# One core, attention and mixture of experts: the first layer norm's transposes by DMA, its bias by DMA, and the last row maxima among the attention units

## The reference

```python
x = x + xattn(layernorm(x), ctx_768, Wq, bq, Wk, bk, Wv, bv, Wo, bo)   # 16 heads of 16, softmax over 64 keys
x = x + ffn(layernorm(x), gate_w, shared and expert weights)           # shared SwiGLU + top 2 of 8 experts
```

## Time and profile before

| | |
|---|---|
| time, median of 3 runs (lowest to highest) | 719.77 us (718.18 to 723.15) |
| profiled execution, its own time | 715.89 us |
| its span, first to last instruction | 713.9 us |
| mean granted TensorE clock, as a share of 2.4 GHz | 0.912 |
| busy: PE, DVE, ACT, POOL | 614.5, 440.9, 346.4, 394.1 us |

### The profile page before, as it was taken

How to read it: one execution, slowest core, us unless ns; L and a number is a source line. 1 busy time by engine, 2 the same in 40 slices (tenths; PEclk the granted TensorE clock), 3 DMA queues, 4 the chain that set the end, 5 groups by cost and what they waited for, 6 DMA issues and landing times.

```text
span 713.9 us, 15571 instructions
## 1 busy us (share of the span) xinstructions
PE 614.5 (86%) x5294; PEld 416.7 (58%) x5294; DVE 440.9 (62%) x925; ACT 346.4 (49%) x561; POOL 394.1 (55%) x325
## 2 busy tenths in 40 slices
PE   4687668899978888977599899999999999999990
PEld 2243233566546554544356578877878787878780
DVE  5857886687787745779996644544454444454450
ACT  3797457787759763453224433333343333333330
POOL 5579687987864102121304446465756665666643
PEclk9899885598768998998989999999999999999996
DMA  8500000134212559434314766466656655656533
GB/s 262 176 2 1 0 1 1 32 70 107 42 39 46 141 150 248 142 100 115 96 59 131 159 91 105 69 106 92 106 85 99 103 99 92 108 93 107 91 46 37
DMA packets 103819, 65.08 MB, mean 91 GB/s; under 512 B 78594, under 2 KB 96964, under 8 KB 103748
## 3 DMA queue, kind: packets, MB, share of 16 engines
q1 hardware_dynamic: 88916, 40.86, 24.7%
q0 software_dynamic: 14832, 23.24, 19.3%
HBM read 29.47 MB, written 17.96 MB: 66 GB/s over the span
## 4 chain that ended last, share of the span: by engine, by line
PE 60%; DVE 20%; ACT 6%; issue 5%; DMA 3%; SPq 3%; POOL 2%; POOLq 0%; DVEq 0%; ACTq 0%
PE bank L1414 58%; DVE arena L966 3%; SPq L493 2%; DVE bank L1019 2%; DMA out<-w_stage,map_i 2%; DVE hidden L1299 2%; ACT arena L818 1%; PE bank L1764 1%; DVE arena L1276 1%; DVE arena L1272 1%; POOL arena L583 1%; ACT arena L733 1%; DVE x_sb L1355 1%; DVE bank L1305 1%; DVE arena L931 1%
## 5 line engine op out<-in xcount | busy, mean ns | idle before, releaser
L1414 PE MATMUL bank<-arena 128*128 128x34 f16 (+6 forms) x1284 | 138.1, 253 | 27.3 <-DVE bank L1019 11.4
L1414 PE MATMUL bank<-qx,arena 128*128 128x256 f16 (+1 forms) x1584 | 157.5, 288 | 3.2 <-ACT hidden L793 2.6
L674 POOL DMA_INDIRECT out<-w_stage,map_i x71 | 114.4, 1611 | 71.4 <-DMA out<-w_stage,map_i 32.6
L1414 PEld LDWEIGHTS bank<-qx,arena 128*128 (+1 forms) x1584 | 126.7, 101 | 25.4 <-issue 10.2
L1414 PEld LDWEIGHTS bank<-arena 128*128 128x128 f16 (+2 forms) x1284 | 74.3, 108 | 78.1 <-issue 47.3
L661 POOL DMA_INDIRECT qx<-rows_d,map_i x71 | 71.8, 1011 | 76.6 <-DVE lane_w L1375 33.7
L1383 DVE TENSOR_TENSOR hidden<-bank,hidden 128x512 f32<-128x512 f32 x71 | 49.1, 692 | 104.3 <-ACT hidden L900 104.3
L1414 PE MATMUL bank<-qx,w_sh 128*128 128x512 f16 x384 | 95.7, 399 | 19.8 <-DVE hidden L1299 17.7
L900 ACT ACTIVATE hidden<-bank 128x512 f32<-128x512 f32 x71 | 42.4, 597 | 129.4 <-PE bank L1414 129.4
L1414 PE MATMUL bank<-arena,w_stage 128*128 x852 | 104.6, 273 | 0.6 <-DVE w_stage L1402 0.4
L1414 PE MATMUL bank<-arena,qx 128*128 (+1 forms) x316 | 84.4, 390 | 14.3 <-DVE arena L966 12.6
(11 more groups left out here) (185 smaller groups left out, 725.1 us busy)
## 6 DMA issues: line engine op xcount, KB each, us to landing
w_stage<-in_w_all SPq DMA_DIRECT2D x27, 512.0 KB, 4.4
x_sb<-in_x SPq DMA_DIRECT2D x8, 512.0 KB, 8.1
rows_d<-arena SPq DMA_DIRECT2D x8, 512.0 KB, 4.0
out<-x_sb POOLq DMA_DIRECT2D x8, 512.0 KB, 5.6
qx<-rows_d,map_i POOLq DMA_INDIRECT x71, 3.1
qx<-qx SPq DMA_TRANSPOSE x71, 3.1
out<-w_stage,map_i POOLq DMA_INDIRECT x71, 3.9
arena<-arena SPq DMA_TRANSPOSE x32, 2.5
```

The costliest lines, as they stand in the source:

```text
L674: pool.indirect_dma_start(out=out, out_offset=bass.IndirectOffsetOnAxis(ap=map_i[:, 1, i:i + 1], axis=0), in_=y_sb[:, r], in_offset=None, ...
L1414: return pe.matmul(o, a, b, start=first, stop=last, skip_group_check=not check)
```

## The change

- Groups 2 to 7 of the first layer norm are transposed by DMA from SP (24 `dma_start_transpose`, four a group) straight from `xn_hl`, which holds high and low half side by side and has three buffers in place of two, into `xn_t`. TensorE's transposes and ScalarE's copies remain for groups 0 and 1. SP issues these DMAs ahead of the first four weight loads.
- Scale and shift come in four chains in place of three, and `k_h` is cast after the third. ScalarE normalises three groups ahead in place of two.
- `add_bo` is a DMA from GpSimd's queue that adds the broadcast `bo` from DRAM to `x_sb`; the broadcast through TensorE goes.
- The low halves of `k`, `wo` and `v` are made on GpSimd in place of VectorE. Three of the four low key blocks move into units 0 to 2.
- 48 row maxima are taken ahead of the flag in place of 56; scores 18 to 47 rotate over four banks. Maxima 48 to 55 come in units 0 and 1, four each; 56 to 63 in units 3 to 10, one each, through bank 7. `copy_max` and `max_t` of the last groups move to later units, and so do three weight splits.

```diff
--- before.py
+++ after.py
...
@@ -347,10 +348,45 @@
         block = ctx.enter_context(nc.Block())
 
         N_CONST = 28
-        N_K, N_Q, N_V = 5, 3, 9
-        CHAIN_OF = (1, 2, 2, 2, 3, 3, 3, 3)
-        SCORED = (0, 0, 8, 18, 29, 40, 48, 56)
-        MAX_BANK = (6, 6, 6, 6, 6, 6, 7, 6)
+        N_K, N_Q, N_V = 5, 2, 9
+        CHAIN_OF = (1, 2, 3, 3, 4, 4, 4, 4)
+        SCORED = (0, 2, 8, 16, 24, 32, 40, 48)
+        XN_BY_PE = 2
+        WIDE_FROM, WIDE_TO = 18, 48
+        LATE_MAX = 56
+
+        def max_bank(n):
+
+            return 6 if n < NG - 2 else 7
+
+        def score_bank(j):
+
+            if j >= LATE_MAX:
+                return 7
+            if WIDE_FROM <= j < WIDE_TO and j % 4 >= 2:
+                return j % 2
+            return 4 + j % 2
+
+        def scores_read_for(j):
+
+            if j >= LATE_MAX:
+                return j
+            return j - 3 if WIDE_FROM <= j < WIDE_TO else j - 1
+
+        def xn_transposed(eng, n):
+
+            if n < XN_BY_PE:
+                eng.wait_ge(xt_ready, n + 1)
+            else:
+                eng.wait_ge(xn_got[n % 2], 16 * GT * (n // 2))
+
+        def late_scores(u):
+
+            if u < 2:
+                return range(LATE_MAX - 8 + 4 * u, LATE_MAX - 4 + 4 * u)
+            if 3 <= u < 11:
+                return range(LATE_MAX + u - 3, LATE_MAX + u - 2)
+            return range(0)
 
...
+
+            for n in range(XN_BY_PE, NG):
+                sp.wait_ge(xnl_ready, n + 1)
+                sp.wait_ge(q_ready, HF * (n - 1))
+                for t in range(GT):
+                    sp.dma_start_transpose(xn_t[:, n % 2, :, :, bass.ts(t, P)].rearrange("p s h t -> p (s h) t"),
+                                           xn_hl[:, n % 3, t].rearrange("p a c -> p (a c)")
+                                           ).then_inc(xn_got[n % 2], 16)
...
             def normal_low(n):
 
                 pool.wait_ge(xnh_ready, n + 1)
-                if n >= 2:
-                    pool.wait_ge(xt_ready, n - 1)
-                pool.tensor_tensor(xn_l[:, n % 2], xn[:, n % 2], xn_h[:, n % 2], ALU.subtract).then_inc(xnl_ready, 1)
+                pool.tensor_tensor(xn_hl[:, n % 3, :, 1], xn[:, n % 2], xn_hl[:, n % 3, :, 0],
+                                   ALU.subtract).then_inc(xnl_ready, 1)
 
             def add_bo(n):
 
-                xg = x_sb[:, bass.ts(n, GT), :]
-                pool.tensor_tensor(xg, xg, bo_bc.unsqueeze(1).to_broadcast([P, GT, C]),
-                                   ALU.add).then_inc(bo_added, 1)
+                pool.wait_ge(xn_ready, n + 1)
+                pool.dma_start(x_sb[:, bass.ts(n, GT), :],
+                               bo.rearrange("(a b c) -> a b c", a=1, b=1).to_broadcast([P, GT, C]),
+                               accum_op=ALU.add).then_inc(bo_added, 16)
...
             def keys(c, b):
 
-                pool.wait_ge(kh_ready, c + 1)
+                pool.wait_ge((kh_ready, kl_ready)[c], 1)
...
+            def values_low(h2):
+
+                r = slice(h2 * KV, (h2 + 1) * KV)
+                vf = v_f[r].rearrange("p b (j h d) -> p b j h d", h=2, d=D)[:, :, :, h2, :]
+                vh = v_hh[r].rearrange("p b (j h d) -> p b j h d", h=2, d=D)[:, :, :, h2, :]
+                pool.tensor_tensor(v_blk_l[r, :, :, h2 * D:(h2 + 1) * D], vf, vh,
+                                   ALU.subtract).then_inc(vblk_ready, 1)
+
             pool.wait_ge(const_ready, N_CONST)
             normal_low(0)
             pool.wait_ge(wq_hi, 1)
             pool.tensor_tensor(wq_hl[:, 1], wq_f, wq_hl[:, 0], ALU.subtract).then_inc(wq_lo, 1)
             keys(0, 0)
             normal_low(1)
-            pool.wait_ge(bo_copied, 1)
+            normal_low(2)
             for n in range(NG):
                 query_low(n)
+                if n + 3 < NG:
+                    normal_low(n + 3)
                 if n < B - 1:
                     keys(0, n + 1)
-                elif n < 2 * B - 1:
-                    keys(1, n - B + 1)
-                if n + 2 < NG:
-                    normal_low(n + 2)
-                if n >= 2:
-                    add_bo(n - 2)
-            for n in range(NG - 2, NG):
+                if n == 2:
+                    pool.tensor_tensor(k_l, k_f, k_h, ALU.subtract).then_inc(kl_ready, 1)
+                if n == 3:
+                    keys(1, 0)
+                if n == 4:
+                    pool.wait_ge(wo_hi, 1)
+                    pool.tensor_tensor(wo_hl[:, 1], wo_f, wo_hl[:, 0], ALU.subtract).then_inc(wo_lo, 1)
+                if n == 5:
+                    pool.wait_ge(vh_ready, 1)
+                if n in (5, 6):
+                    pool.wait_ge(ql_ready, HF * (n + 1))
+                    values_low(n - 5)
+                    pool.wait_ge(vblk_ready, n - 4)
                 add_bo(n)
...
 
             def unit(u):
-                if u == 1:
+                if u < B - 1:
+                    keys(1, u + 1)
+                if u == 3:
                     low_weight(1)
...
-                if n >= 2:
-                    act.wait_ge(xt_ready, n - 1)
-                act.copy(xn_h[:, n % 2], xn[:, n % 2]).then_inc(xnh_ready, 1)
+                if n >= 3:
+                    xn_transposed(act, n - 3)
+                act.copy(xn_hl[:, n % 3, :, 0], xn[:, n % 2]).then_inc(xnh_ready, 1)
...
             normal(0)
             project_inputs()
+            normal(1)
             copy_xt(0)
-            normal(1)
+            normal(2)
             for n in range(NG):
                 query(n)
-                if n + 1 < NG:
-                    copy_xt(n + 1)
+                if n == 0:
+                    copy_xt(1)
                 if 1 <= n <= B:
                     copy_v(n - 1)
-                if n + 2 < NG:
-                    normal(n + 2)
+                if n + 3 < NG:
+                    normal(n + 3)
             act.wait_ge(scale_ready, 1)
+            act.wait_ge(vblk_ready, 2)
...
                 if known(u, 0):
                     cast_p(u, RT - 1)
-                if u == 0:
-                    for q in range(3):
-                        split_hi(q)
+                if 1 <= u < 4:
+                    split_hi(u - 1)
...
             scale_and_shift(slice(0, GT), moments1(0))
-            moments1(1)
+            scale_and_shift(slice(GT, 2 * GT), moments1(1))
             moments1(2)
             ins = moments1(3)
+            scale_and_shift(slice(2 * GT, 4 * GT), ins)
             dve.wait_ge(k_copied, HF)
             dve.tensor_copy(k_h, k_f).then_inc(kh_ready, 1)
-            dve.wait_ge(kh_ready, 1)
-            dve.tensor_tensor(k_l, k_f, k_h, ALU.subtract).then_inc(kh_ready, 1)
-            scale_and_shift(slice(GT, 4 * GT), ins)
             for g in range(4, NG):
                 ins = moments1(g)
...
-            def row_max(n):
-
-                for i in range(GT):
-                    for hf in range(HF):
-                        dve.wait_ge(smax_ready, HF * (GT * n + i) + hf + 1)
-                        dve.tensor_reduce(m_raw[:, n % 2, i, bass.ts(hf, HH)],
-                                          bank[4 + hf][:, :].rearrange("p (h k) -> p h k", h=HH),
-                                          AX.X, ALU.max).then_inc(smax_used, 1)
+            def row_max(j):
+
+                t, hf = divmod(j, HF)
+                n, i = divmod(t, GT)
+                dve.wait_ge(smax_ready, j + 1)
+                dve.tensor_reduce(m_raw[:, n % 2, i, bass.ts(hf, HH)],
+                                  bank[score_bank(j)][:, :].rearrange("p (h k) -> p h k", h=HH),
+                                  AX.X, ALU.max).then_inc(smax_used, 1)
+
+            def clip_max(n):
+
                 dve.wait_ge(smax_used, HF * GT * (n + 1))
...
-            def split_values(h2):
+                                bank[max_bank(n)][:, 0:256].bitcast(F16)).then_inc(mt_copied, 1)
+
+            def high_values(h2):
 
...
                 vh = v_hh[r].rearrange("p b (j h d) -> p b j h d", h=2, d=D)[:, :, :, h2, :]
-                dve.tensor_copy(v_blk_h[r, :, :, c], vh).then_inc(vblk_ready, 1)
-                dve.tensor_tensor(v_blk_l[r, :, :, c], vf, vh, ALU.subtract).then_inc(vblk_ready, 1)
-
-            for n in range(NG - 1):
-                row_max(n)
+                dve.tensor_copy(v_blk_h[r, :, :, h2 * D:(h2 + 1) * D], vh).then_inc(vblk_hi, 1)
+
+            for n in range(NG - 2):
+                for j in range(HF * GT * n, HF * GT * (n + 1)):
+                    row_max(j)
+                clip_max(n)
                 if n >= 2:
                     copy_max(n - 2)
                 if n == 2:
-                    split_output_weight(wo_f, wo_hl)
+                    dve.wait_ge(v_loaded, 16 * N_V)
+                    dve.tensor_copy(wo_hl[:, 0], wo_f).then_inc(wo_hi, 1)
                 if n == 3:
-                    split_output_weight(gate_f[:, :, :], gate_hl[:, :, :, :].rearrange("p h s e -> p s h e"))
```

(72 more changed lines are left out.)

40 lines of the change are left out of this document (11 added, 29 removed).

## The result

| | before | changed |
|---|---|---|
| time, median (lowest to highest) | 720.56 us (718.18 to 723.15) | 732.5 us (726.99 to 735.77) |
| ratio of the times, 95% interval | | 1.0165 (1.0115 to 1.0215) |
| span of the profiled execution, mean granted clock | 713.9 us, 0.912 | 725.2 us, 0.893 |

A forecast was written before the change was run, and what follows sets the result against it. It took the layer-norm chain, then VectorE, to bound the front, TensorE the units, and GpSimd's queue as the front's next bound. Front -20.5 plus units +13.3 made -7.2 us: 713 us, range 703 less 1 to 726.

The forecast's parts named there:

- a sum of 2.1: Units 0 to 4: units 0 and 1 unchanged, unit 2 +0.5, unit 3 +1.2, unit 4 +0.4 us.
- The rival by which its cost goes by rows at 6.3 us: Front: bias DMA issue on GpSimd costs 6.3 us, 5.4 above that taken; front gives 1, time 732; chance 0.15.
- my path was wrong: Units 5 to 10: VectorE waits for score, takes maximum, rows_of, normalise; 7.2 us a unit at full clock, 8.9 at half.
- the middle between the two clocks, 49.3: Units 5 to 10: between 44.4 us at full clock and 54.2 at half, against 38.1 before.
- The term was 11.2: Units 5 to 10: us lost to late maxima, 49.3 against 38.1.
- 20.5: Front: us gained up to the first clip of unit 0, forecast at 81.5 in place of 102.04.
- a bad end: Front gives only 10 us: bias issue at 1.6, clock at half, transposes landing at 7.9 instead of 2.6.
- My own sign of being wrong: Front: forecast is wrong if query 7 begins after 80 us.
- my sum: Front: GpSimd's queue from 22.9 us, 41.4 of work plus about 2 of waits; low half 7 ends at 66.3.
- by my path: Front after low half 7: transposes 6.5, query 7 with scores 6.4, then 0.69 and 1.64 us until first clip.
- the fourth rival's reading of the stage: VectorE stays the front's bound, its own work ending at 83, within error of 81.5; no chance given.
- both bad ends: Front gives only 10 us and 18.2 are given back in the units: 728, called unlikely together.

The follow-up runs named there:

- Experiment 1: Changed kernel with the late row maximum behind rows_of and normalise: 712.97 us, 0.9915 of before; behind rows_of only: 713.33 us, 0.9927.
- experiment 2: Changed kernel with the bias DMAs left out and bo not added: 720.06 us, 1.0018 of the kernel before.
- experiments 3 and 6: max_t one group later in the changed kernel: 732.87 us; also late maximum behind rows_of and normalise, GpSimd bias adds where idle: 706.25 us, or no bias: 696.2 us.
- e5_three: Changed kernel with late maximum behind rows_of and normalise, max_t one group later, no bias added: 696.2 us, 0.9647 of before.
- e1_rows_first: Changed kernel with the late row maximum of units 3 to 10 behind rows_of and normalise: 712.97 us, 0.9915 of before.
- e6_bias_gpsimd: Changed kernel with late maximum behind rows_of and normalise, bias added by GpSimd in groups 4 to 7: 717.36 us, 0.9951 of before.
- e7_best: As e6_bias_gpsimd, with max_t one group later: 715.82 us, 0.9981 of before.
- e11_by_sync: Changed kernel with the bias transfers as plain writes over x_sb from SyncE's queue, none issued by GpSimd: 727.09 us.
- e10_placed: As e7_best, with GpSimd's bias adds moved to where it stood idle, some in units 4, 15 and 16: 706.25 us, 0.9778 of before.

## Why the prediction was wrong, point by point

**Right.** Late maxima in units 3 to 10 lengthen units 5 to 10, because VectorE waits for the score ahead of work that TensorE needs. Units 0 to 4 lose little (0.6 against a sum of 2.1), but that is partly luck: units 0 and 1 took 1.2 us less, not the same, and unit 3 took 2.1 more, not 1.2. What follows from unit 11 on has the same work, but units 11 to 14 took 3.0 us less at a granted clock of 0.91 in place of 0.77, for which I had no term. The bias DMA takes some 0.8 to 1.0 us of GpSimd's queue, as taken: its row says 1.29, but the next instruction starts 0.82 after it (64.85 to 65.67). The rival by which its cost goes by rows at 6.3 us is out; that its number, 732, was met is chance.

**The step that failed most: what stands behind the late maximum.** I had TensorE wait for `normalise` and for the next clip, and priced a unit as VectorE's chain from the end of the subtracts: 7.2 us at full clock, 8.9 at half. The consumer that counts is `project`, which waits for `rows_of`, in the very same unit. I named "`rows_of` and `normalise`" as queued behind the new wait, and for the first did not look up who waits for it. With it TensorE's work splits into two pieces with VectorE between: 0.70 + 0.14 + 4.09 + 0.69 + 0.60 + 0.14 + 4.15 = 10.5 us (an issue time of 0.02 left out), 9.3 where one piece runs at the higher clock. With both pieces at the higher clock it would be 7.4, an estimate: 2.86 for the 45 matmuls, and 2.26 from `project` to the next clip, as in unit 12 (202.68 to 204.94). So at the higher clock my path was wrong by only 0.2 us a unit, and at the lower by 1.6 (10.5 against 8.9), since it is TensorE's own work that stands in the chain and grows with the clock. Experiment 1 fits: residual first, and the units are back at 40.5 to 41.2. I also took the middle between the two clocks, 49.3; TensorE, standing still twice in a unit, got 0.61, near the lower end. The term was 11.2 and measured 21.5; of the 10.3 us between, by the same estimate, about half is the path and half the clock.

**Second: the front, 7.0 in place of 20.5.** My own sign of being wrong, query 7 beginning after 80, came true: it began at 86.3. Three things, the first of which I had only as a bad end.
- The bias DMAs' traffic. I costed their issue, and the transposes' landing at the median 2.6 with 5.3 us as the bad end. They landed after 5.2 in the median, and the bias DMAs themselves after 10.5: 512 KB written from one DRAM row, where the 512 KB loads of weights landed after 4.4. Together with the next point they cost 8.9 us (experiment 2). The Trainium skill, "DMA: Bandwidth & Descriptors", section "Issuing engines are not separate DMA queues", named the right mechanism, and the trace agrees: transposes from SyncE's queue went from 2.5 to 5.2 us with transfers issued by GpSimd beside them.
- VectorE's clips of 4 to 11 us. No row of before had one (its longest, 1.34 us, was beside GpSimd too), and I had no term for it.
- `max_t` behind the scores instead of ahead. The diff shows the two lines swapped; I passed over them. It is worth 5.8 us once the bias is out (experiments 3 and 6).

With both out, e5_three has its first clip at 80.4, where I had 81.5. That the two are so close is luck in part. GpSimd was done with low half 7 at 62.5, and my sum, less its 3.6 us for the bias issues that e5_three doesn't have, gives 62.7; but by my path the first clip would then follow at about 78. VectorE, busy without a pause, ends last there, so the fourth rival's reading of the stage was right, in this kernel at least. The change could have given the front what I counted; it brought its own obstacles.

**The sum.** -20.5 + 13.3 was forecast; measured is -7.0 + 0.6 + 21.5 - 3.0 - 0.8 = +11.3 in the traces, and +11.9 by the medians. The range ended at 726 because I held both bad ends together for unlikely. They came together, each beyond its end: 7 against 10 in the front, 22 against 18.2 in the units.

**Open.** What exactly keeps VectorE's instruction over SBUF waiting for 4 to 11 us isn't settled. It was seen beside GpSimd's queue running without a pause, with DMA issues in it (front) and without (unit 3 of e6_bias_gpsimd and e7_best), and not in e11_by_sync, where GpSimd has pauses; but in e10_placed the same split beside GpSimd without a pause took only 2.17 us. The Trainium skill, "SBUF — State Buffer", section "Who interferes with whom", has VectorE in its two-port modes and GpSimd shut each other out of a shared pair of ports for a whole instruction, and has a VectorE instruction with two inputs in SBUF, as the split has, contend with GpSimd's reads. The kinds of instruction that stood are such as it names; the length does not agree, since the stalls of 10 us outlast four GpSimd instructions and more, so a single such lock does not explain them. That the clock fell because TensorE stood still, and not for another reason, is not shown: the longer idle times and the lower clock (0.61 against 0.87) come and go together between the changed kernel and e1_rows_first, and were not tried apart.

## What to carry to other kernels

For every instruction that a new wait is put ahead of, look up each engine that waits for it, not only the one you have in mind, and look for it within the same turn of the loop: one maximum of 0.69 us put ahead of a residual cost some 19 us in six units. Ask too whose work the new chain holds: if it is TensorE's, price it at both levels of its clock. Moving work from an engine to a DMA moves it beside the other DMAs, so a cheap issue doesn't settle its price; here transfers that landed after 10 us held up those beside them, although nobody needed their own result before unit 5. And a unit of work that fits nowhere at once can often be dealt out to where the engine is idle: the same eight adds gave 715.8 us in a bunch ahead of the units and 706.3 spread out (0.998 and 0.978 of the kernel before beside each).

## What the runs showed of the hardware

- Accumulating 512 KB from DRAM in a GpSimd-issued DMA costs 1.29 us of issue against 0.79 for the plain write; reading one DRAM row for every partition lands after 9.5 to 10.5 us, from an SBUF tile after 6.2.
- Crossbar transposes beside such transfers land after 5.2 us in the median and up to 12.2, alone after 2.5.
- VectorE instructions over SBUF of 0.3 to 1.2 us stood for 4.4 to 11.5 us beside an unbroken run of GpSimd instructions, in some traces; in others the same ones took 0.3 to 2.3 us.
